# Value projection of an attention layer on one NeuronCore: from channel-major with transposes to token-major with the weights moving

## What is computed

```python
xn = _layernorm(x)
qkv = xn @ attn_qkvw + attn_qkvb          # 1024 -> 3 * 1024
q, k, v = ...                             # 32 heads of 32 channels
ctx = softmax(q @ k.T / sqrt(32)) @ v     # per head, 2048 x 2048
z = (xn @ A_w.T) * gate                   # 1024 -> 512, gate from a top-16 router
out = x + ctx @ attn_ow + attn_ob + (z @ B_w.T) * 2.0
```

## Time and profile before

| | |
|---|---|
| time, median of 3 runs | 2595.83 us (2594.63 to 2596.72) |
| the profiled execution, its own time | 2596.82 us |
| its span, first to last instruction | 2595.0 us |
| mean granted TensorE clock | 0.992 of full speed |
| busy: PE, weight loads, DVE, ACT, POOL | 98%, 64%, 58%, 47%, 62% |
| `project_inputs`, `attend`, `project_output` end at about | 741, 2310, 2595 us |

### The profile page before, as it was taken

One profiled execution on the slowest core, in us unless ns is written; L12 is line 12 of the kernel. 1 busy time (PEld: TensorE's weight loads), 2 busy tenths in 40 slices (PEclk: granted clock), 3 DMA queues, 4 the chain that ended last, 5 costly groups with the idle time before them and its releaser, 6 DMA issues. The chain is left out here.

```text
span 2595.0 us, 34876 instructions
## 1 busy us (share of the span) xinstructions
PE 2532.0 (98%) x13032; PEld 1648.6 (64%) x13032; DVE 1512.7 (58%) x2522; ACT 1218.1 (47%) x2299; POOL 1607.3 (62%) x529
## 2 busy tenths in 40 slices
PE   7999999999989999999999999999999999979999
PEld 6888888777855555555555555555555555428887
DVE  8511111011658888878878878888888888532222
ACT  3211111111026667666766666666666667750000
POOL 0100111101138999999999999999999999942211
PEclk9999999999989999999999999999999999989999
DMA  4233324222356787787787787787787787633332
GB/s 154 90 122 121 113 110 133 73 73 73 90 154 128 157 169 152 155 169 151 157 165 155 156 166 152 158 166 152 159 164 151 161 167 145 124 107 103 110 111 93
DMA packets 168168, 351.01 MB, mean 135 GB/s; under 512 B 89632, under 2 KB 114720, under 8 KB 137376
## 3 DMA queue, kind: packets, MB, share of 16 engines
q0 software_dynamic: 22320, 162.54, 32.4%
q1 hardware_dynamic: 145712, 186.70, 25.2%
HBM read 122.44 MB, written 63.69 MB: 72 GB/s over the span
## 5 line engine op out<-in xcount | busy, mean ns | idle before, releaser
L991 DVE TENSOR_REDUCE part_max<-ps_b 128x1 f32<-128x512 f32 x1984 | 1213.3, 679 | 276.2 <-PE ps_b L868 276.1
L819 POOL TENSOR_TENSOR psum_p<-psum_p,probs 128x2048 f32<-128x2048 f32 x254 | 1183.5, 4660 | 55.7 <-ACT probs L978 44.3
L978 ACT ACTIVATE probs<-ps_b 128x512 f32<-128x512 f32 x1924 | 973.5, 622 | 366.4 <-PE ps_b L858 363.0
L858 PE MATMUL ps_b<-qp,kp 97*128 97x512 f32 x1344 | 550.5, 413 | 4.6 <-ACT probs L978 4.5
L868 PE MATMUL ps_b<-kp,qp 96*128 96x512 f32 x1344 | 536.9, 401 | 7.1 <-DMA qp<-qk_scr 6.5
L886 PE MATMUL ps_b<-probs,vh 128*32 128x512 f32 x3848 | 466.8, 598 | 0.0
L264 POOL TENSOR_TENSOR wlo<-wraw,whi 128x1024 fp32r<-128x1024 f32 x29 | 69.5, 2399 | 624.5 <-ACT whi L398 624.5
L858 PEld LDWEIGHTS ps_b<-qp,kp 97*128 97x128 f32 x1344 | 251.8, 188 | 233.6 <-issue 135.3
L297 PE MATMUL ps_a<-xhi,whi 128*128 128x512 f32 (+1 forms) x800 | 320.1, 400 | 1.1 <-DVE elo L487 0.9
L297 PE MATMUL ps_a<-xlo,whi 128*128 128x512 f32 (+1 forms) x800 | 317.3, 397 | 0.0
L297 PE MATMUL ps_a<-xhi,wlo 128*128 128x512 f32 (+1 forms) x800 | 317.2, 396 | 0.0
(11 more groups left out here) (97 smaller groups left out, 2004.9 us busy)
## 6 DMA issues: line engine op xcount, KB each, us to landing
psum_q<-probs POOLq DMA_DIRECT2D x155, 1024.0 KB, 7.8
qk<-qk_scr SPq DMA_DIRECT2D x66, 256.0 KB, 7.1
qk_scr<-ehi SPq DMA_DIRECT2D x16, 1024.0 KB, 3.9
qk_scr<-elo SPq DMA_DIRECT2D x16, 1024.0 KB, 6.7
kp<-qk_scr SPq DMA_DIRECT2D x63, 256.0 KB, 4.1
qp<-qk_scr SPq DMA_DIRECT2D x63, 256.0 KB, 7.9
wraw<-wcat SPq DMA_DIRECT2D x29, 512.5 KB, 7.5
craw<-cz_scr SPq DMA_DIRECT2D x16, 768.0 KB, 5.0
```

The costliest lines, as they stand in the source:

```text
L819: pool.tensor_tensor(acc[:, :], first[:, :], tile(h, t)[:, :], ALU.add).then_inc(pool_done, 1)
L858: pe.matmul(ps[:, n % ST_BANKS, :], kp[s][0:PACK + 1, t * P:(t + 1) * P], qp[s][0:PACK + 1, b * NQ:(b + 1) * NQ], start=True, stop=True).t ...
L978: act.activation(tile(h, t)[:, b * NQ:(b + 1) * NQ], ps[:, n % ST_BANKS, :], ACT.Exp, scale=SCALE).then_inc(exp_done, 1)
L991: dve.tensor_reduce(part_max[hn % 2][:, tn, b:b + 1], ps[:, ring_bank(u), :], AX_X, ALU.max) \
```

## The change

The value blocks leave the list of blocks: `wcat` holds the router, query, key and z weights only, so that z is now blocks 17 to 20. Values are made in a stage of their own between block 16 and z, as four groups: two halves of the output channels (512 each) by two halves of the tokens (8 tiles of 128). A group is 8 steps, one for each tile `k` of input channels. In a step a piece of W_v of 128x512 moves, and the eight token tiles of xn stand one after the other, three matmuls each, into eight PSUM banks. So the result has tokens on the partitions, and nothing is transposed. The pieces (`wv`, 32 of 256 KB; every piece is loaded twice, once for each half of the tokens) go through four half slots of `wraw`, `whi` and `wlo` (`v_slot`). DVE takes a finished bank with the bias `vbias`, which SP loads broadcast over the partitions at the start, into `elo`, and SP stores four tiles at a time to `v_scr`, now [2048 tokens][1024 channels]. `qp0` and `kp0` no longer wait for the value stage, which does not touch `ehi`: SP loads them within it. `load_values` reads the same 2048 pieces of 128 bytes from the new layout: neighbouring tokens lie 4096 bytes apart, and one partition's 16 pieces 512 KB apart (512 bytes apart before).

The value stage on PE, ACT, POOL and DVE:

```diff
+            for n in range(V_STEPS):
+                g, k = divmod(n, KT)
+                pe.wait_ge(vlo_done, n + 1)
+                for j in range(V_TILES):
+                    if k == 0 and g >= 1:
+                        pe.wait_ge(v_taken, V_TILES * (g - 1) + j + 1)
+                    elif k == 0 and j < QB:
+                        pe.wait_ge(lo_done, quarter(Z0 - 1, j))
+                    t = V_TILES * v_place(g)[1] + j
+                    for i, (xx, w) in enumerate(((xhi, whi), (xlo, whi), (xhi, wlo))):
+                        last = pe.matmul(ps[:, j, :], xx[:, k, t * P:(t + 1) * P], v_slot(w, n),
+                                         start=(k == 0 and i == 0), stop=(k == KT - 1 and i == 2))
+                    if k == KT - 1:
+                        last.then_inc(v_ready, 1)
+                if k < KT - 1:
+                    last.then_inc(v_ready, 1)
...
+            def round_v(n):
+                act.wait_ge(vw_loaded[n % V_SLOTS], 16 * (n // V_SLOTS + 1))
+                if n < V_SLOTS:
+                    act.wait_ge(mm_ready, product(Z0 - 2 + n // 2, 3))
+                else:
+                    act.wait_ge(v_ready, v_step(n - V_SLOTS))
+                act.activation(v_slot(whi, n), v_slot(wraw, n), ACT.Copy).then_inc(vhi_done, 1)
...
+            for n in range(V_STEPS):
+                pool.wait_ge(vhi_done, n + 1)
+                pool.tensor_tensor(v_slot(wlo, n), v_slot(wraw, n), v_slot(whi, n).bitcast(F32), ALU.subtract) \
+                    .then_inc(vlo_done, 1)
...
+            dve.wait_ge(vbias_loaded, 16)
+            for n in range(V_GROUPS * V_TILES):
+                g, j = divmod(n, V_TILES)
+                half = v_place(g)[0]
+                dve.wait_ge(v_ready, v_tile(g, j))
+                dve.wait_ge(stored[j // CHUNK], QK_STORED + 16 * g)
+                dve.tensor_tensor(v_out[:, j, :], ps[:, j, :], vbias[:, half * NQ:(half + 1) * NQ], ALU.add) \
+                    .then_inc(v_taken, 1)
```

SP, from the last pair of key blocks on, and the read in `attend`:

```diff
+            for u, blk in pair(QK_BLOCKS // 2 - 1):
+                sp.wait_ge(lo_done, quarter(blk, 3))
+                store_qk(blk, u)
+                for n in range(2 * u, 2 * u + 2):
+                    load_v(n)
+            for n in range(V_SLOTS, V_STEPS):
+                sp.wait_ge(vlo_done, n - V_SLOTS + 1)
+                load_v(n)
+                if n == V_SLOTS + 1:
+                    sp.wait_ge(gate_stored, 16)
+                    for u in range(2):
+                        load_gates(u, u)
+                if n == V_SLOTS + 3:
+                    for u in range(2):
+                        sp.wait_ge(stored[u], QK_STORED)
+                    for row, dst in ((0, qp0), (D, kp0)):
...
+                if n % KT == 0 and n // KT >= 2:
+                    for q in range(2):
+                        store_v(2 * (n // KT) - 4 + q)
-            sp.wait_ge(vtr_ready, QB * V_BLOCKS)
...
-                s, c = h % SLOTS, h % 4 * HD
-                sp.dma_start(vh[s][:, :, :], v_scr[h // 4].rearrange("p (t c) -> p t c", c=P)[:, :, c:c + HD]) \
+                s = h % SLOTS
+                sp.dma_start(vh[s][:, :, :], v_scr[:, h * HD:(h + 1) * HD].rearrange("(t p) c -> p t c", p=P)) \
```

More of the change, by code:

```diff
@@ L217, in _ @@
             sp.dma_start(gate_scr, gate_t).then_inc(gate_stored, 16)
-            with sp.Fori(1, QK_BLOCKS // 2) as i:
+            with sp.Fori(1, QK_BLOCKS // 2 - 1) as i:
                 after_qk(i)
-            sp.wait_ge(gate_stored, 16)
-            for u in range(2):
[L222 to L231, removed]
@@ L232, in _, with load_v @@
-            for u in range(2):
-                sp.wait_ge(stored[u], 32 * QK_BLOCKS // 2)
-            sp.wait_ge(vtr_ready, QB * V_BLOCKS)
[L235 to L238, removed]
+            def load_v(n):
+                half, k = v_place(n // KT)[0], n % KT
+                sp.dma_start(v_slot(wraw, n), wv[k * P:(k + 1) * P, half * NQ:(half + 1) * NQ]) \
+                    .then_inc(vw_loaded[n % V_SLOTS], 16)
@@ L239, in _ @@
+            for u in range(2):
+                sp.wait_ge(vlo_done, V_STEPS - 2 + 2 * u)
+                load_w(Z0 + u, (u + 1) % 2)
+            for q in range(2 * V_GROUPS - 4, 2 * V_GROUPS):
+                store_v(q)
             for b in range(Z_BLOCKS):
@@ L435, in part @@
                             round_w(blk + 1, u, i + 2)
-                        q_part(u, blk, nb, rounded)
-            for u, blk in pair(0):
+                        q_part(u, blk, nb)
+            for u, blk in pair(QK_BLOCKS // 2 - 1):
+                act.wait_ge(stored[u], 32 * (QK_BLOCKS // 2 - 1))
                 for nb in range(QB):
[L440 to L447, removed]
-            with act.Fori(QK_BLOCKS // 2, (QK_BLOCKS + V_BLOCKS) // 2) as i:
-                part(i, False)
-            for blk in range(Z0 + 1, BLOCKS):
+                    if nb == 1 and u == 0:
+                        round_w(blk + 1, u, QK_BLOCKS // 2 + 1)
+                    elif nb == 1:
+                        round_v(0)
+                        round_v(1)
+                    q_part(u, blk, nb)
+            for n in range(2, V_STEPS):
+                round_v(n)
+            for blk in range(Z0, BLOCKS):
+                if blk < Z0 + 2:
+                    act.wait_ge(v_ready, v_step(V_STEPS - 3 + 2 * (blk - Z0)))
                 round_w(blk, blk % 2, blk // 2 + 1)
```

90 lines of the change are left out of this document (64 added, 26 removed).

## The result

| | before | after |
|---|---|---|
| median | 2596.27 us (2594.63 to 2597.19, 4 runs) | 2572.09 us (2571.43 to 2573.11, 4 runs) |
| the profiled execution, its own time and span | 2596.82, 2595.0 us | 2571.77, 2570.0 us |

A forecast was written before the change was run, and what follows sets the result against it. PE, busy for 2532 of 2595 us, was taken to bound the kernel. Terms of -19.8, -4.5 and +0.6 summed to -23.7 us, forecasting a median of 2572 us, range 2566 to 2581.

The forecast's parts named there:

- The transposes: Value blocks: 128 transposes and the waits in front of them leave PE's queue, 199.0 to 179.2 us, -19.8 us.
- The pace: New value stage: 768 matmuls at the key blocks' 0.2333 us each; at 0.228, as in project_output, 4 us less.
- rival (b): Value stage: moving weights run as fast as in project_output or faster, total 2568 us or below; chance 0.06.
- The wait for `kq0_loaded`: First z block: PE's stop for the qp0 and kp0 loads (2.9 us) and its lower clock (1.6) go, -4.5 us.
- the first term: The sum's term for the transposes and their waits in the value blocks, -19.8 us.
- The third step: Start of the value stage: the third weight piece is ready at 440.0, PE at 439.4, +0.6 us, bounds 0 and 3.
- What costs nothing: Value stage and start: DVE's banks, ACT's and POOL's work, gate loads and the bias load are covered, no cost.
- The value loads of the heads: Start of attend: scattered 128-byte pieces taken as 0 us; twice the landing time would cost 3 to 5, upper end +5.
- (a): Start of value stage or attend worse: third piece late with clock (+4) or slow first value load (+5), 2576 to 2582; chance 0.12.
- (d): Attention heads: slow scattered value loads hold up every head; one us a head gives 2603 us; chance 0.02.
- (c): Value stage: short waits and bank changes lower PE's clock, 0.427 us a matmul, 149 us more, 2721 us; chance 0.02.
- (e): Value stage: not bound by PE, weights late at every step, needing over 5.6 us of ACT or POOL a piece; chance under 0.01.

The follow-up runs named there:

- no_transposes: The kernel before with its value transposes left out (DVE copies ehi to elo, so attention works on wrong values): 2575.8 us, ratio 0.9926.
- runs 5 to 9: Five runs, four on the kernel after's or key blocks' matmul order, standing operand, banks or piece size, one giving project_output the value stage's order: 2571.6 to 2576.1 us.
- kq0_late: The kernel after with the six loads of qp0 and kp0 moved back behind the last store of the values: 2573.9 us.
- both_halves: The kernel after with its value stage in project_output's order, 128x1024 pieces in two slots, first two loaded early, gate, qp0 and kp0 loads spread: 2576.1 us.
- pieces_early: The kernel after with its first four pieces of W_v loaded ahead of the last two key blocks' stores: 2571.6 us, ratio 0.9905.
- banks_in_turn: The kernel after with two token tiles' matmuls alternating in the value stage, so consecutive matmuls write different PSUM banks: 2571.9 us.
- standing_twice: The kernel after with a token tile's three value matmuls reordered so the same operand stands for two in a row: 2571.6 us.
- before_aligned: The kernel before with only wraw allocated behind stage, so whi, wlo, elo and stage start on a multiple of 64 bytes: 2581.1 us, ratio 0.9946.

## Why the prediction was right, point by point

- **The transposes, -19.8.** Right: the stage is 180.2 us by starts, 179.3 without its one stop, and `no_transposes` gets 179.2 from the other side.
- **The pace, 0.2333 with 0.228 as the lower end.** The number was right, the reason wrong twice. The key blocks do not change the standing operand with each matmul, as the prediction says: L297 lets `whi` stand for two, as project_output does with its tile. And the standing operand has no part in it, as it is loaded anew for every matmul in any case, nor have the banks (runs 5 to 9). The pace was the key blocks' because the new stage reads the same two badly placed buffers. Had the change happened to move them onto a multiple of 64, the kernel would have been some 15 us faster than forecast, for a cause that neither the sum nor rival (b) names. The Trainium skill (TensorE: Matmul & The Clock Gate, Back-to-back issue gap) gives 216 ns for 512 columns, as the gap of an isolated matmul; here even well-placed operands show 227 in a stream.
- **The wait for `kq0_loaded`, -4.5.** The z blocks gave 4.6. But the account of it was too simple: `kq0_late` shows that in the new stage, loads issued late would have cost 1.4 us (1.8 by the medians). About 3 of the 4.5 were the later issue in the old blocks, behind two stores and a load of weights, and the clock that fell behind the longer stop. It is no overlap with the first term: without the transpositions alone the stop stays, and costs 4.1.
- **The third step, +0.6 with bounds 0 and 3.** 0.92: the piece landed at 437.4 instead of 437.9, but PE was done with step two at 438.5, not 439.4, since the stage began 0.9 earlier than in the profile before; ACT's and POOL's 0.63 and 1.29 add up to 1.92, where 1.89 was estimated. It needed no clock term; that the upper bound was right to hold one is shown by `both_halves`, where a stop of 2.51 us has 1.4 us of slow matmuls behind it. `pieces_early` takes the stop away.
- **What costs nothing.** DVE, ACT, POOL, the gates behind the sixth piece and the bias load show no stop. The bias takes 8.3 us to land, about twice the estimate, yet PE's stop at the end of the stage of x is over at 80.01 with that load and at 79.82 in `no_transposes` without it, 79.16 in `kq0_late` with it: within the scatter.
- **The value loads of the heads, 0 with +5 above.** 0: landings 8.0 against 8.1, and from the last matmul of z to the last of `attend` it takes 1573.9 us in both profiles (735.95 to 2309.81 before, 711.66 to 2285.53 after). Rivals (a), second half, and (d) fall. The cover was larger than the prediction says: 13.6 us against a landing of 8.1 leave two thirds more free, not one third, and twice as long would have cost 2.6 us, not 3 to 5.
- **(c), the clock.** It stays at 1.00 in all 768 matmuls, also where the bank changes with every one (`banks_in_turn`). The only fall in a value stage, in `both_halves`, stands behind a stop of 2.51 us, and the clock is back up for the rest of a stage that changes bank with every matmul. The Trainium skill's depth-cycling (the same page, A second HAM failure mode: psum-queue depth-cycling) is not seen in the value stage of any of these runs.
- **(e).** ACT waits 111 of 160 us for PE, and POOL 111 for ACT.

## What to carry over

Before asking how an order of work changes a matmul's pace, compare where its operands start: moving one oddly sized buffer behind the others took 6.7 ns off each of some 2100 matmuls of the key and value products, and was worth 15 us, more than half of what the change itself brought. A stop at a load is made of when it is issued and of what it lands behind, so a change that takes stores and loads out of the queue in front of the issue already takes part of the stop, and an experiment that takes out only one part of a change, as `no_transposes` does, shows which part it was not. And a term taken from the nearest row can be right for a reason that is not the one given: name what the two places have in common, operand addresses included.

## What the runs showed of the hardware

- A 128x512 matmul in fp32r whose weights operand starts 32 bytes beyond a multiple of 64 comes every 0.2333 us; with both operands on a multiple of 64, every 0.2267. It holds for the standing and for the moving operand, and the order of banks or of standing operands changes neither pace. Other offsets, and an offset in x, were not tried.
- PE loads the standing operand before every matmul, also where the one before had the same: 768 loads for the 768 matmuls of `standing_twice`.
- Stops of PE of 0.75, 0.96, 1.20 and 2.26 us in full matmul streams left the granted clock up; behind stops of 2.51 (`both_halves`), 2.75 (before), 3.20 (`before_aligned`) and 3.97 us (`no_transposes`) six to twelve matmuls came 0.43 us apart. Why some executions show the same fall at 90 us, where the stream is the same, stays open.
- Scattering the 2048 pieces of 128 bytes of a value load over 8 MB instead of one block changed its landing by nothing (8.0 against 8.1 us).
